# A gated cross-attention block with mixture of experts: row matmul behind tile 1, gathers one add earlier, a weight unit later, three one-hot rows on GpSimd

## The reference, cut to what matters

```python
x = x + jnp.tanh(g_xattn[0]) * _L0_xattn_ref(_layernorm(x), ctx, ...)   # top-2 of 64 sets per token
...
xf = _layernorm(x).reshape(-1, 256)
logits = xf @ gate_w + gate_b
top_val, top_idx = jax.lax.top_k(logits, 2)
gate_score = jax.nn.softmax(top_val, axis=-1)
comb = jnp.einsum('tk,tke->et', gate_score, onehot) * alpha[:, None]
# for each of the 8 experts, over all tokens (w is 0 where not picked):
h = jax.nn.gelu(xf @ w1 + b1, approximate=False)     # 256 -> 1024
y = h @ w2 + b2                                      # 1024 -> 256
acc = acc + y * w[:, None]
...
out = x + jnp.tanh(g_ffn[0]) * acc
```

## Time and profile before

| | us |
|---|---|
| median of 3 runs | 321.17 (318.71 to 322.14) |
| the profiled execution | 317.56 |
| its span, first to last instruction | 315.7 |
| TensorE busy (matmuls) | 255.0, 81% of the span |
| VectorE busy | 213.7, 68% |
| ScalarE busy | 178.8, 57% |
| GpSimd busy | 142.9, 45% |
| mean granted TensorE clock | 0.898 |

### The profile page before, as it was taken

One profiled execution on the slowest core, in us unless ns is written; L12 is line 12 of the kernel. 1 busy time (PEld: TensorE's weight loads), 2 busy tenths in 40 slices (PEclk: granted clock), 3 DMA queues, 4 the chain that ended last, 5 costly groups with the idle time before them and its releaser, 6 DMA issues.

```text
span 315.7 us, 9126 instructions
## 1 busy us (share of the span) xinstructions
PE 255.0 (81%) x3075; PEld 237.8 (75%) x3075; DVE 213.7 (68%) x701; ACT 178.8 (57%) x495; POOL 142.9 (45%) x119
## 2 busy tenths in 40 slices
PE   3999351242679989999999699999999999999920
PEld 3998341231669978999998699999999999999910
DVE  3898999896656785866786667677768555555400
ACT  2145878775516766567666646856685454545410
POOL 2121168945210566346456633635464646562330
PEclk9999755555659999999999999999999999999985
DMA  6999999974400244444444655443544445446310
GB/s 172 347 371 378 377 375 380 367 265 172 102 19 20 52 68 87 85 71 71 68 73 67 88 83 69 61 79 70 87 70 85 76 80 86 72 67 69 36 20 13
DMA packets 47262, 41.04 MB, mean 130 GB/s; under 512 B 23570, under 2 KB 43795, under 8 KB 47091
## 3 DMA queue, kind: packets, MB, share of 16 engines
q1 hardware_dynamic: 39088, 29.75, 32.1%
q0 software_dynamic: 7488, 10.39, 21.7%
q10 hardware_dynamic: 642, 0.33, 0.4%
HBM read 26.10 MB, written 9.37 MB: 112 GB/s over the span
## 4 chain that ended last, share of the span: by engine, by line
PE 27%; DMA 26%; issue 15%; DVE 11%; POOL 4%; ACT 3%; POOLq 0%; ACTq 0%; DVEq 0%; SPq 0%
DMA out_dram<-xn,add_at 23%; PE bank L614 14%; PE bank L630 12%; POOL out_dram L1508 2%; DMA xs<-xrows,fetch_at 2%; POOL xs L1500 2%; DMA xTp<-xs 1%; DVE wreg L1059 1%; ACT rows L875 1%; DVE xs L1029 1%; DVE rows L1050 1%; DVE earlier L1103 1%; ACT xn L777 1%; DVE gmark L1093 1%; DVE rows L1423 1%
## 5 line engine op out<-in xcount | busy, mean ns | idle before, releaser
L614 PE MATMUL bank<-xTp,wreg 128*128 128x128 f16 x1872 | 157.4, 223 | 5.4 <-DMA xTp<-xs 4.6
L630 PE MATMUL bank<-wreg,rows 128*128 x936 | 151.2, 274 | 0.0
L614 PEld LDWEIGHTS bank<-xTp,wreg 128*128 x1872 | 132.9, 100 | 14.6 <-DMA xTp<-xs 6.4
L875 ACT ACTIVATE rows<-bank,maskbias 128x128 f32<-128x128 f32 x312 | 88.6, 369 | 59.7 <-PE bank L614 32.5
L1508 POOL DMA_INDIRECT out_dram<-xn,add_at x39 | 65.9, 1690 | 98.6 <-ACT xn L883 63.2
L630 PEld LDWEIGHTS bank<-wreg,rows 128*128 128x128 f16 x936 | 79.4, 98 | 4.1
L1423 DVE TENSOR_SCALAR rows<-rows 128x512 f16<-128x512 f32 x78 | 36.8, 472 | 49.8 <-ACT rows L875 41.0
L1500 POOL DMA_INDIRECT xs<-xrows,fetch_at x39 | 46.7, 1196 | 29.1 <-issue 21.2
L1425 DVE SCALAR_TENSOR_TENSOR rows<-rows 128x512 f16<-128x512 f32 x78 | 54.0, 693 | 2.7
L1288 DVE SCALAR_TENSOR_TENSOR wreg<-wreg (+1 forms) x16 | 36.7, 2293 | 14.2 <-ACT wreg L804 11.9
L883 ACT ACTIVATE xn<-xn,maskbias 128x256 f32<-128x256 f32 x39 | 20.0, 513 | 32.3 <-DVE xn L1414 32.1
(11 more groups left out here) (201 smaller groups left out, 205.9 us busy)
## 6 DMA issues: line engine op xcount, KB each, us to landing
wreg<-in_L_ffn_fc_w_dram SPq DMA_DIRECT2D x16, 1024.0 KB, 13.6
xrows<-rows SPq DMA_DIRECT2D x4, 528.0 KB, 6.5
xs<-in_x_dram SPq DMA_DIRECT2D x4, 512.0 KB, 8.7
out_dram<-xs SPq DMA_DIRECT2D x4, 512.0 KB, 8.1
xs<-in_L_ffn_fc_b_dram SPq DMA_DIRECT2D x1, 1024.0 KB, 6.1
xs<-xrows,fetch_at POOLq DMA_INDIRECT x39
out_dram<-xn,add_at POOLq DMA_INDIRECT x39
xTp<-xs SPq DMA_TRANSPOSE x38
```

Source lines behind the costliest of these rows:

```text
L614: mm = pe.matmul(put, w, xT[:, i % NX, x_part, k, :], start=(k == 0 and n == 0), stop=(k == KC - 1 and n == 2))
L630: mm = pe.matmul(yb, h, w, start=(c == 0 and n == 0), stop=(c == FC - 1 and n == 2))
L875: op = act.activation(h32[i % 2][:, f * P:(f + 1) * P], bank[2 * (i % 2) + half][:, c * P:(c + 1) * P], ACT.Gelu, bias=b1cur[:, i % NX, f: ...
```

## The change

Five edits. The row matmul stands behind tile 1 instead of tile 0, and VectorE's work for it is cut into `table_cols` (behind tile 0's split), `table_fetch` and `table_rest` (between the halves of tile 1's split) and `table_adds` (behind tile 1's split). GpSimd issues gather i+5 in front of add i instead of gather i+4, and waits for `add_at` only before the first add. Unit 3 is cast behind tile 3 instead of tile 2. VectorE's parts of units 2 and 3 stand between the halves of the split of the next tile. Of group 3's `at_col` rows, ScalarE makes five and GpSimd three.

```diff
-        units_of_tile = {1: (2,), 2: (3,)}
+        units_of_tile = {1: (2,), 3: (3,)}
...
# TensorE
-                pe.wait_ge(onehots, min(g + 1, NG - 1))
+                pe.wait_ge(onehots, g + 1)
...
                 tile(i, ws[i + 2], ws[i + 1], ws[i])
-                if i == 0:
+                if i == 1:
                     pe.wait_ge(cols_ready, 2)
                     pe.matmul(bank[6][:, 0:TILES], tokens_at[:, :], is_col[:, :], start=True, stop=True).then_inc(fetch_ps, 1)
...
# ScalarE: the rows come in pieces of one or two
-            column_rows(2, (2, 3))
-            column_rows(3, (0, 1, 2, 3))
+            column_rows(2, ((4, 5), (6, 7)))
+            column_rows(3, ((0, 1), (2, 3), (4,)))
...
# VectorE
+            def table_cols():
+                v.tensor_reduce(per_tile[:, 0, :], found_a, AX.X, ALU.add).then_inc(vec_step, 1)
+                at = done.up()
+                v.tensor_tensor(begun, ends, by_tile(of_expert[:, 2, :]), ALU.mult).then_inc(vec_step, 1)
+                done.up()
+                v.wait_ge(vec_step, at)
+                v.tensor_tensor(col_f[:, :], per_tile[:, 0, :], iota_t[:, :], ALU.add).then_inc(vec_step, 1)
+                v.wait_ge(vec_step, done.up())
+                v.tensor_scalar(is_col[:, :], col_f[:, :], iota_p[:, 0:1], None, ALU.is_equal).then_inc(cols_ready, 1)
+
+            def table_fetch():
+                v.wait_ge(fetch_ps, 2)
+                v.tensor_copy(fetch_at[:, PER_RANK:TILES], bank[6][:, PER_RANK:TILES]).then_inc(fetch_ready, 1)
...
             def table_adds():
-                v.wait_ge(fetch_ps, 2)
-                v.tensor_copy(fetch_at[:, PER_RANK:TILES], bank[6][:, PER_RANK:TILES]).then_inc(fetch_ready, 1)
                 v.wait_ge(fetch_ready, 2)
...
                 split(i, 0)
+                if i == 1:
+                    table_fetch()
+                    table_rest()
+
+                for k in units_of_tile.get(i - 1, ()):
+                    if k < 4:
+                        weights_lo(k, unit_regions(k))
                 split(i, 1)
                 if i == 0:
-                    table_rest()
+                    table_cols()
+                if i == 1:
                     table_adds()
                 for k in units_of_tile.get(i, ()):
-                    weights_lo(k, unit_regions(k))
+                    if k >= 4:
+                        weights_lo(k, unit_regions(k))
...
# GpSimd
             column_rows(2, range(0, 4))
+            column_rows(3, range(5, 8))
...
-            pool.wait_ge(add_at_ready, 1)
+            fetch_rows(NXG)
             for i in range(TILES):
-                if i + NXG < TILES:
-                    fetch_rows(i + NXG)
+                if i + NXG + 1 < TILES:
+                    fetch_rows(i + NXG + 1)
+                if i == 0:
+                    pool.wait_ge(add_at_ready, 1)
                 add_tile(i)
```

More of the change, by code:

```diff
@@ L768, in route_exp, with column_rows @@
                 op.then_inc(gexp_ready, 1)
-            def column_rows(g, tiles):
+            def column_rows(g, pieces):
                 act.wait_ge(slots_ready, g + 1)
@@ L774, in column_rows @@
                     act.wait_ge(row_ready, g)
-                for q in tiles:
-                    for j in (2 * q, 2 * q + 1):
+                for piece in pieces:
+                    for j in piece:
                         op = act.activation(at_col[g][:, j, :], iota[:, :], ACT.Square, bias=place_f[:, g, 0, j:j + 1], scale=-1.0)
                     op.then_inc(squared, 1)
[L779 to L784, removed]
+                squares_done[0] += len(pieces)
+                for n, piece in enumerate(pieces):
+                    act.wait_ge(squared, squares_done[0] - len(pieces) + n + 1)
+                    t = g * GT + piece[0] // 2
+                    part = at_col[g][:, piece[0]:piece[-1] + 1, :].rearrange("p j q -> p (j q)")
+                    op = act.activation(part, part, ACT.Relu, bias=token[:, t:t + 1], scale=minus_token[:, t:t + 1])
                 op.then_inc(act_onehots, 1)
@@ L1241, in table_found @@
                 v.wait_ge(vec_step, done.up(3))
+            def table_cols():
[10 more added lines that the diff above has]
+                v.tensor_copy(fetch_at[:, PER_RANK:TILES], bank[6][:, PER_RANK:TILES]).then_inc(fetch_ready, 1)
             def table_rest():
-                v.tensor_reduce(per_tile[:, 0, :], found_a, AX.X, ALU.add).then_inc(vec_step, 1)
-                v.tensor_tensor(begun, ends, by_tile(of_expert[:, 2, :]), ALU.mult).then_inc(vec_step, 1)
                 v.tensor_reduce(per_tile[:, 1, :], found_b, AX.X, ALU.add).then_inc(vec_step, 1)
-                v.wait_ge(vec_step, done.up(3))
-                v.tensor_tensor(col_f[:, :], per_tile[:, 0, :], iota_t[:, :], ALU.add).then_inc(vec_step, 1)
                 v.tensor_reduce(per_tile[:, 2, :], begun, AX.X, ALU.add).then_inc(vec_step, 1)
                 v.wait_ge(vec_step, done.up(2))
-                v.tensor_scalar(is_col[:, :], col_f[:, :], iota_p[:, 0:1], None, ALU.is_equal).then_inc(cols_ready, 1)
                 v.scalar_tensor_tensor(out=real[:, :], in0=iota_t[:, :], scalar=-float(P), in1=per_tile[:, 1, :],
@@ L1472, in column_rows @@
                 pool.wait_ge(slots_ready, g + 1)
+                if g == NG - 1:
+                    pool.wait_ge(row_ready, g)
                 for j in picked:
@@ L1476, in column_rows @@
                                             ALU.is_equal, ALU.mult)
-                    if j == (GT * 2 if g < NG - 2 else GT) - 1:
+                    if j == (GT if g == NG - 2 else GT * 2) - 1:
                         op.then_inc(onehots, 1)
```

## The result

The changed kernel takes 306.00 us (median of 4 runs, 305.95 to 306.14) against 321.65 (4 runs, 318.71 to 325.47): a ratio of 0.9543, 95% interval 0.9478 to 0.9608. Forecast were 308.3 us and 304.5 to 315.5. The profiled execution took 306.14 with a span of 304.3, so 11.4 us less than the profiled one of before (317.56, 315.7); 12.0 were forecast on that scale.

A forecast was written before the change was run, and what follows sets the result against it. TensorE was taken as the bound from first fc1 to last fc2. 7.1 + 5.2 - 0.6 + 0.3 = 12.0 us off the 321.17 median gave 309.2; less 0.9 for run spread, 308.3 us, range 304.5 to 315.5.

The forecast's parts named there:

- Row matmul and clock: Row matmul behind tile 1: tile 1 starts at 84.30, runs at full clock, tile 2 at 88.3; 7.1 us won.
- The split in 4.5 and 2.6: Tile 1 on TensorE: 4.5 us won by starting earlier, 2.6 us by keeping the full clock.
- VectorE's order: VectorE around the row matmul: tile 1's second split half ends 1.3 us before TensorE wants it (the cover); cost nothing.
- The lead: Gather i+5 in front of add i: all four late waits for transposes go, 5.2 us won.
- step 4: Unit halves apart on VectorE: one new fc2 wait at tile 5, 0.6 us lost, bounds 0 and 2.3.
- the rival: Gathers' lead does nothing, since lateness comes from colliding transfers and moves along: 314.4 us, chance 0.12.
- One-hot rows: Three column rows moved to GpSimd before the table matmuls: 0.3 us won, bounds 0.6 won and 0.9 lost.
- The 3.6 us between the profiled execution and the median: Profiled run of before under the median, part probably late gathers; a quarter, 0.9 us, counted as won.
- the lower bound: Range's low end, 304.7 taken as 304.5: 0.6 of new wait, 0.3 of one-hot rows, 2.7 of run spread.
- the three bounds (1.3, 1.7, 1.2): Upward bounds: row matmul's move 1.3, unit halves 1.7, one-hot rows 1.2; added to the middle ones for 315.5.
- if TensorE still idles between tiles: Sign on TensorE's timeline: any idle time left between tiles would make the prediction wrong.
- The slower rival: Adds become the bound in the tile loop; at 1.0 us more per add, 326.2 us, chance 0.04.

The follow-up runs named there:

- experiment 4: Kernel before with 70 matmuls of unread result in front of TensorE's wait for the row matmul behind tile 0: 317.03 us, ratio 0.9960.
- experiment 1: Kernel before with only gather i+5 issued in front of add i, the rest as before: 312.34 us, ratio 0.9854.
- 2: Changed kernel with GpSimd's loop as before, gather i+4 in front of add i: 314.31 us, ratio 0.9838 to the kernel before.
- experiment 7: Kernel before with the low part of each unit made by four VectorE instructions instead of one: 319.04 us, ratio 0.9987.
- experiment 3: Changed kernel with all eight at_col rows of group 3 on ScalarE again: 307.05 us.
- experiment 12: Changed kernel with unit 3 behind tile 2, unit 0's low part in four instructions, and 44 idle matmuls before TensorE's wait for gather 0: 306.43 us.
- experiment 6: Changed kernel with 44 matmuls of unread result in front of TensorE's wait for gather 0: 310.07 us.
- 10: Changed kernel with one more gather of lead, gather i+6 in front of add i: 306.76 us, ratio 0.9672 to the kernel before.
- 11: Changed kernel with unit 3 behind tile 2 again and unit 0's low part alone in four instructions: 305.91 us, ratio 0.9637 to the kernel before.
- 9: Changed kernel measured once more in another session, nothing changed: 306.07 us, ratio 0.9648 to the kernel before.
- 8: Changed kernel with the low part of each unit in four VectorE instructions: 307.52 us.

## Why the prediction was right, point by point

1. *Row matmul and clock, 7.1 forecast, 6.77 measured.* Of the 7.02 by which tile 2 is earlier, 0.25 is the front part's (tile 0 at 78.89 against 79.14) and belongs to point 5. Tile 1 waited 0.33 for its transpose, inside the 1.3 allowed; the reading that its traffic was over at 83 and its rows there before 84.30 did not hold. The split in 4.5 and 2.6 is shown by experiment 4, not only argued.
2. *VectorE's order.* The copy for the gathers came at 88.66 (89.1 forecast), gather 4 at 89.12 (90.2; it stood 0.46 behind the copy, not 1.1), the split of tile 1's second half ended at 92.3 as worked out, tile 4 came without a wait. The cover held.
3. *The lead, 5.2 forecast, 5.24 measured.* Between the starts of the matmuls the four late tiles of before lost 1.23, 0.93, 0.47 and 2.61, and nothing of it is left. The gain behind tile 2 is 4.62 and not 5.24 because of step 4 and because of new small gaps, of which the longest is 0.46 in front of tile 36; the profile calls it issue and no run explains it. Experiments 1 and 2 show that it is the lead. The reason given against the rival, that gather 17 itself was late, carried little: experiment 7 took such gathers away and the waits stayed.
4. *Unit halves, 0.6 lost forecast, 0.45 measured*, at the place named. VectorE's rows:

```profile
104.42 2.29 DVE L1297 SCALAR_TENSOR_TENSOR wreg<-wreg  x1
...
109.04 2.29 DVE L1297 SCALAR_TENSOR_TENSOR wreg<-wreg  x1 [1.28 <-ACT wreg L806]
...
111.72 0.42 DVE L1432 TENSOR_SCALAR rows<-rows 128x512 f16<-128x512 f32 x1
```

and TensorE's:

```profile
112.23 0.50 PE L615 MATMUL bank<-xTp,wreg 128*128 128x128 f16 x6
113.01 0.49 PE L631 MATMUL bank<-wreg,rows 128*128 x3 [0.28 <-DVE rows L1434]
```

With tile 4 at 98.98, unit 3's low part ends at +7.7, unit 4's begins at +10.05, the split at +12.7, as worked out (+7.65, +10.1). The forecast left out the fc1 chunk of 0.33 that stands in front of that fc2 group, and with it would have been 0.3. The edit itself wins nothing that a run shows: with unit 3 at tile 2 again (experiment 5) the stretch from tile 2 to the end of fc2 is 200.9 us in the trace, against 201.6.
5. *One-hot rows, 0.3 won forecast, 0.17 measured* against experiment 3 (0.25 against the kernel before, of which 0.09 was there at the first square already). VectorE's one-hots released the table matmuls, as said, but 0.4 later than they would have ended alone. So "nothing is added for it" was wrong in size: the rows of before compared only the low rows. The rule of the Trainium skill (SBUF — State Buffer, "Who interferes with whom"), by which each GpSimd row would shut VectorE out for its whole length, 2.5 us in all, is not borne out either; the runs show a sixth of that.
6. *The 3.6 us between the profiled execution and the median, of which a quarter was taken:* this is the term that was mis-sized, and why 306.0 came and not 308.3. The medians fell by 15.65 and the profiled executions by 11.4, so 4.2 of it went and not 0.9. The quarter had no working behind it, and that the result fell inside the range is owed to the lower bound, which took the whole 3.6. The profile of before was one of the lucky ones: of the 41 runs of that kernel 6 were shorter than its 317.56. That the waits of that kernel differ from run to run is argued from the spreads, since no trace of a long run of it was kept. With the lead the kernels spread over 0.2 to 3.6 us (0.6 in experiment 1), or 4.7 and 6.1 with idle matmuls on top (12 and 6); without it over 6.1 (2 and 7) to 11.5 (before, last session), some of them with more runs.

Not all of the spread is late gathers. In the traces of 6, 7, 10 and 11 the clock is 0.50 from 24 to 30 us, deep in the front part, where it is 1.00 in all others; here 11 and then the changed kernel:

```profile
24.00:30.00 6.00, 6.00 (x31) 5.80 (x31) 5.28 (x23) 1.83 (x7) 1.13 (x1) 0.50 1.06 377
24.00:30.00 6.00, 5.75 (x51) 5.24 (x51) 5.36 (x25) 3.16 (x10) 1.01 (x1) 1.00 1.06 376
```

Tile 0 starts at 79.85 to 80.40 in those four and at 78.25 to 79.49 in the others. The mean clock of each run tells the same: in 9, 10 and 11 the runs at 0.889 to 0.891 took 307.0 to 309.3 us, those at 0.901 to 0.906 took 304.7 to 306.5. What makes the clock fall there no run shows. The kernel before has such runs as well, but its runs at 0.896 to 0.899 alone still spread from 315.6 to 323.0.

How the range's upper end of 315.5 comes about stays unclear: the three bounds (1.3, 1.7, 1.2) are added to "the middle ones", which are not named, and on top of 308.3 they make 312.5. And by the letter of its own sign, "if TensorE still idles between tiles", the prediction would have failed: TensorE idles 0.33 in front of tile 1 and 0.30 in front of tile 36. The sign was put too sharply; the idle time that was to go is gone.

The prediction called adds 5.4 and more apart a sign of being wrong; from add 0 at 94.76 to add 38 at 293.73 they are 5.24 apart. The slower rival did come nearer: 24 adds of 39 were released by the landing of the add before, 18 before the change.

## What to carry to other kernels

Measure how far ahead of its use each transfer is issued and how much it needs: where the two are equal, waits can differ from run to run, and a profile of a good run may understate them. Give one slot of lead in the issue order, then stop. A wait at the head of a dense stretch of matmuls is paid twice when it is long enough for the clock to fall, so move small helper matmuls behind the next tile, and do not make TensorE early in front of an arrival that does not come earlier with it.

## What the runs showed of the hardware

- TensorE's granted clock: kept over 2.90 us without matmuls (experiment 12), lost over 4.02 (experiment 6) and over 4.49 (before). It fell some 2.0 us after the last matmul in experiment 6 and 3.1 us after it in before. At half clock the same thirty matmuls took 3.36 to 3.38 us, at full clock 1.85.
- GpSimd's writing of an indirect DMA is held beside VectorE's scalar_tensor_tensor of 2.29 us with both inputs in SBUF: gathers of 1.0 us took up to 3.08, an add of 1.6 took 3.47; with the instruction in four (experiments 7 and 8) no gather took over 1.55.
- Where TensorE waited for a tile, it started 7.2 to 10.5 us behind the start of its gather in before and 6.5 to 9.2 in experiment 7, where no gather was held. Adds started 4.2 us apart at the closest in before and 4.4 in the changed kernel.
